# Graph attention on one core: row units put between masks and scores of a step

## The reference

```python
qkv = layer_norm(x, g1, be1) @ w_qkv
q, k, v = (qkv[:, 0], qkv[:, 1], qkv[:, 2])          # after reshape(n, 3, HEADS, HEAD_DIM)
scores = jnp.einsum('nhd,mhd->hnm', q, k) * SCALE
scores = jnp.where((adj != 0)[None, :, :], scores, -jnp.inf)
attn = jax.nn.softmax(scores, axis=-1)
out = jnp.einsum('hnm,mhd->nhd', attn, v).reshape(n, DIM)
x = x + out @ w_proj + b_proj
h2 = layer_norm(x, g2, be2)
return x + jax.nn.gelu(h2 @ w1 + b1) @ w2 + b2
```

## Time and profile before

| | |
|---|---|
| median of three runs | 1814.01 us (1806.6 to 1814.49) |
| profiled execution | 1812.5 us, its span 1810.7 us |
| granted TensorE clock over the span | 0.976 |
| TensorE matmuls | 1673.6 us, 92% |
| VectorE | 1421.2 us, 78% |
| ScalarE | 1300.8 us, 72% |
| GpSimd | 1179.4 us, 65% |
| chain that ended last | TensorE 71%, ScalarE 15%, issue 10%, VectorE 2% |

### The profile page before, as it was taken

How to read it: one execution, slowest core, us unless ns; L and a number is a source line. 1 busy time by engine, 2 the same in 40 slices (tenths; PEclk the granted TensorE clock), 3 DMA queues, 4 the chain that set the end, 5 groups by cost and what they waited for, 6 DMA issues and landing times.

```text
span 1810.7 us, 48122 instructions
## 1 busy us (share of the span) xinstructions
PE 1673.6 (92%) x17826; PEld 553.9 (31%) x17826; DVE 1421.2 (78%) x4495; ACT 1300.8 (72%) x1443; POOL 1179.4 (65%) x1113
## 2 busy tenths in 40 slices
PE   6989999999999999999999999999999999999985
PEld 3422222323223232323223232323223232233223
DVE  6888889877898779887888779887898778987601
ACT  4547777677776777777776877677776877777771
POOL 5944586568855787468855688458865688457441
PEclk9869999999999999999999999999999999999996
DMA  7710035202450035301360035300351024500000
GB/s 214 168 42 2 25 108 110 54 1 66 135 100 2 13 106 117 66 1 54 114 133 2 1 100 124 77 2 26 123 106 47 2 77 124 77 2 1 8 7 6
DMA packets 168846, 115.24 MB, mean 64 GB/s; under 512 B 139298, under 2 KB 149156, under 8 KB 168612
## 3 DMA queue, kind: packets, MB, share of 16 engines
q1 hardware_dynamic: 157860, 103.78, 23.7%
q10 hardware_dynamic: 10752, 8.39, 1.6%
HBM read 74.39 MB, written 4.19 MB: 43 GB/s over the span
## 4 chain that ended last, share of the span: by engine, by line
PE 71%; ACT 15%; issue 10%; DVE 2%; DMA 1%; POOL 0%; SPq 0%; ACTq 0%; DVEq 0%; POOLq 0%
PE pv_ps L1023 19%; PE ring_ps L960 14%; PE score_ps L1127 12%; PE score_ps L1112 12%; ACT probs L728 12%; PE score_ps L1046 2%; PE ring_ps L1080 2%; PE ring_ps L1071 2%; PE ring_ps L1056 2%; PE ring_ps L1062 2%; PE score_ps L1036 2%; PE score_ps L984 2%; ACT q_stack L612 1%; ACT hidden L689 1%; DMA adj_in<-adj 1%
## 5 line engine op out<-in xcount | busy, mean ns | idle before, releaser
L763 DVE CUSTOM_DVE_ANT_0 masked_out<-ring_ps,row_mask 128x512 bf16<-128x512 f32 x2048 | 1310.3, 687 | 163.2 <-PE ring_ps L960 129.4
L728 ACT ACTIVATE probs<-score_ps,score_scale 128x1024 f32<-128x1024 f32 x1024 | 1089.0, 1113 | 358.0 <-PE score_ps L1127 350.4
L517 POOL TENSOR_TENSOR probs<-probs,keep 128x1024 int32<-128x1024 int32 x256 | 604.4, 2362 | 324.3 <-ACT probs L728 313.3
L1023 PE MATMUL pv_ps<-probs,v_ones 128*17 128x512 f32 x4096 | 539.2, 599 | 0.5 <-POOL probs L517 0.4
L960 PE MATMUL ring_ps<-k_stack,q_stack 51*64 51x512 f16 x4096 | 493.3, 397 | 13.3 <-DVE row_max L763 12.8
L1127 PE MATMUL score_ps<-q_stack,k_stack 51*64 51x512 f16 x4096 | 373.5, 391 | 26.6 <-ACT probs L728 7.4
L1112 PE MATMUL score_ps<-mask_t,ident_bf 64*64 64x512 bf16 x3072 | 276.1, 387 | 60.9 <-ACT probs L728 14.6
L960 PEld LDWEIGHTS ring_ps<-k_stack,q_stack 51*64 51x64 f16 x4096 | 165.8, 104 | 454.7 <-DVE row_max L763 401.9
L1127 PEld LDWEIGHTS score_ps<-q_stack,k_stack 51*64 51x64 f16 x4096 | 116.9, 104 | 229.2 <-PE score_ps L1112 181.1
L763 DVE DVE_READ_ACCUMULATOR2_ANT row_max<- 128x1 f32 x2048 | 169.4, 83 | 0.0
L1112 PEld LDWEIGHTS score_ps<-mask_t,ident_bf 64*64 64x64 bf16 x3072 | 92.4, 105 | 211.3 <-ACT probs L728 114.1
(11 more groups left out here) (106 smaller groups left out, 969.6 us busy)
## 6 DMA issues: line engine op xcount, KB each, us to landing
adj_in<-adj SPq DMA_DIRECT2D x128, 512.0 KB, 4.1
xnT_dram<-attn ACTq DMA_DIRECT2D x8, 256.0 KB, 3.9
mask_t<-row_mask SPq DMA_TRANSPOSE x128, 3.4
xq<-xnT_dram ACTq DMA_DIRECT2D x8, 256.0 KB, 2.6
x_res<-x ACTq DMA_DIRECT2D x8, 256.0 KB, 4.4
out<-rows ACTq DMA_DIRECT2D x8, 256.0 KB, 2.6
w_sb<-L_gnn_w SPq DMA_DIRECT2D x2, 256.0 KB
probs<-x SPq DMA_DIRECT2D x1, 256.0 KB, 2.9
```

The source lines that it names most:

```text
L517: nc.gpsimd.tensor_tensor(view, view, keep[:, KEPT.index(m), :].unsqueeze(1).broadcast_to([128, 2, TILE]), ALU.mult).then_inc(probs_masked, 1)
L728: nc.scalar.activation(probs[:, (2 * g + n) % SLOTS, :], score_ps[:, half:half + 2, :].rearrange("p a n -> p (a n)"), ACT.Exp, scale=score ...
L763: nc.vector.tensor_tensor_reduce(out=masked_out[:, place % 3, :], in0=ring_ps[:, place % 3, :], in1=row_mask[:, j, ch * 512:(ch + 1) * 512 ...
L1023: last = nc.tensor.matmul(pv_ps[32 * k:32 * k + HD + 1, :], v_ones[:, block_of(g, b), 2 * p + a, :], probs[:, (2 * g + b) % SLOTS, a * TIL ...
```

## The change

Only the order of TensorE's instructions inside a step changes. Before, two row units stood first, then all masks and scores of both blocks, then two row units, then the values. Now the first masks stand first (masked step only), then two row units, first scores, second masks, two row units, second scores, values. Fills stay behind the values.

```diff
                 for g in range(STEPS):
+                    if c and not pool_step(g):
+                        masks(g, 0)
                     for x in range(UNITS // 2):
                         row(g, x)
-                    if c and pool_step(g):
+                    if c:
                         scores(g, 0)
                         masks(g, 1)
-                        scores(g, 1)
-                    elif c:
-                        masks(g, 0)
-                        masks(g, 1)
-                        scores(g, 0)
-                        scores(g, 1)
                     for x in range(UNITS // 2, UNITS):
                         row(g, x)
+                    if c:
+                        scores(g, 1)
                     if g < LAG and d:
                         weigh_values(i - 1, made_by(i - 1), STEPS - LAG + g)
```

## The result

The changed kernel takes 1893.29 us (median of 4 runs, 1891.82 to 1896.46) against 1814.25 us before; the ratio is 1.044, 95% interval 1.0421 to 1.046. Its profiled execution took 1896.46 us, with a span of 1894.7 us, 84.0 us more than the span of before. The forecast was 1897 us.

A forecast was written before the change was run, and what follows sets the result against it. Taken as bound by latency, with the row chain of 1.35 us a floor in each step. Plain-first steps +11, masked +63, fills -12, -9 and +31 sum to +84 us on 1814: 1898, told as 1897 us; range 1845 to 1932.

The forecast's parts named there:

- Bound: Each step: fourth row unit needs the first's bank, so it cannot start sooner than 1.35 us after the first.
- Part 1: Plain-first step: two row units between second masks and second scores save 0.24 us on paper, and ScalarE's wait there goes.
- Part 2: Before the fourth row unit: TensorE waits 0.65 us instead of 0.18 (masked step) or none; chain taken as 1.37 us.
- Part 3: Behind the fourth row unit: second scores now precede the values, 0.55 us to the values instead of 0.31 to 0.33.
- rival C: Second scores run beside the fourth row unit, 0.43 us to the values instead of 0.55: 1845 us; chance 0.13.
- Part 4: Masked step: first masks ahead of the first row units add 0.22 us no longer hidden under the row chain.
- The fills: 175 steps with other work between values: -12 us behind shift transpositions, -9 behind q or up projections, +31 in others.
- The ends: Stage without row units, paced by ScalarE, left at nothing (-3 to +3 us); start of the program unchanged.
- A sign that read wrong: Profile after, whole kernel: VectorE and ScalarE keep their busy time and lose share.
- A: Faster: fourth row unit isn't held, 0.24 us saved in about 240 plain-first steps, 58 us, 1756 us; chance 0.04.
- B: No change: the row chain takes what the masks gain, or VectorE's earlier start pays it back, 1814 us; chance 0.04.
- D: Clock: pauses of 0.65 us per step drop a tenth of the steps to 1.2 GHz, +115 us, 2010 us; chance 0.05.

The follow-up runs named there:

- Run 3: Changed kernel with VectorE's row maximum over 256 instead of 512 columns of each row unit: 1782.72 us, against the changed kernel's 1893 us.
- run 1: Kernel before with only the first masks of a masked step moved ahead of its first two row units: 1833.1 us, ratio 1.0106.
- run 5: Changed kernel with the second scores ahead of the fourth row unit instead of behind it: 1820.71 us, ratio 1.0042 to the kernel before.
- run 2: Kernel before with only the second scores of each step moved behind the last two row units: 1859.69 us, ratio 1.0257.
- run 9: Kernel before, changed order only behind q or up projections or shift transpositions without VectorE fill, and in the masked step ahead of such a transposition: 1798.99 us.
- run 6: Kernel before with the second scores between third and fourth row unit, first masks left behind the first two row units: 1805.5 us, ratio 0.9965.
- run 4: Kernel before with VectorE's row maximum over 256 instead of 512 columns of each row unit: 1770.95 us, ratio 0.976.

## Why the prediction was right, step by step

**Bound.** The row chain, 0.60 + 0.69 + 0.06 us from the first to the fourth row unit of a step, was named as a floor. It held: 425 of 480 steps after have the fourth unit between 1.32 and 1.38 us, none sooner. Run 3 shows that it is VectorE's duration that sets it: 0.27 us less of that, and the fourth unit comes 0.27 us sooner. The floor presumes that VectorE is free when the first row unit comes; runs 1, 3 and 5 show steps where it was not.

**Part 1, the masks' latency.** Right that it is gained (scores' waits for masks halved), right that it is worth nothing in a plain step, since the time is waited for the row chain instead. Wrong in a detail: waits of masks for ScalarE were said to shrink and stayed (94.7 against 94.4 us).

**Part 2, the cover.** 1.35 to 1.37 us measured, 1.37 taken.

**Part 3, what stands behind the late unit.** 0.55 us measured, 0.55 taken, and run 5 shows it alone: with the scores ahead of the fourth row unit it is 0.33 us again, and 73 us come back. The picture behind the number was not quite right. The four score matmuls don't all come 0.22 us behind the row unit: the group has a record of 0.61 us instead of 0.41. The two matmuls issued last, of which one carries the group's semaphore increment, start at 864.19 beside the row unit, and the two issued first 0.23 us later. So rival C's mechanism exists, but the values need the whole array and follow the later half; it saves nothing.

**Part 4, the first masks.** 0.24 to 0.25 us measured, 0.22 taken. Run 1 shows the part alone at +20 us, less than half of what run 2's part costs, because here the next step gets something back.

**The fills.** All three groups within 3 us of the forecast (-12 for -12, -8 for -9, +34 for +31). The reason given for the first was half of it; run 9 shows the rest.

**The ends.** Left at nothing, they gave -1 us behind the last row unit and some -3 us in the start. The start also differs between the other kernels with the whole row maximum: first values at 128.0 and 129.9 us in the two whose granted clock over the first 122 us was 0.89, at 130.4 to 134.3 us in the rest (0.84 to 0.87). This is why the profiled execution is 1896.5 us where steps alone say 1812.5 + 88 = 1900.5. The steps were 4 us above the forecast and the ends 4 us below it, so that both cancel is luck.

**A sign that read wrong.** VectorE and ScalarE were to keep their busy time. VectorE did within 11 us; ScalarE's rose by 45 us, by records that no longer overlap and not by more work.

**The rivals.** A is out, since no step has the fourth unit sooner than 1.32 us. B is out by the time and by the masked step's +0.42 us. C is out by the 0.55 us of part 3. D is out: granted clock 1.00 from 152 to 1780 us. The rule of the Trainium skill, "TensorE: Matmul & The Clock Gate", section "A second HAM failure mode: psum-queue depth-cycling", that short idle moments between groups of matmuls that cycle through PSUM banks can make the clock swing, is not borne out here: a pause of about 0.6 us in most steps left it at 1.00, the upper level.

## What to carry to other kernels

With a ring of n buffers between two engines, the use n places on can't start sooner than producer's latency + consumer's time + the way back, and later if the consumer has something else in hand. Measure this once (here 1.35 us for three banks) and put as much other work of the producer into that span as it holds; what stands behind the waiting instruction in the same queue is added in series. So the last unit of a burst belongs at the end, with everything that doesn't need it ahead of it. And an order need not be the same in every step: where another engine is late for its own reasons, the order that loses elsewhere can win.

## What was not expected of the hardware

Matmuls that use only half of the array's rows can start ahead of matmuls issued before them that wait for the other half. In the changed kernel two of the second scores do so by 0.23 us (part 3 above). In run 6 the queue is first scores x4, third row unit x2, second scores x4, fourth row unit x2:

```profile
886.34 0.62 PE L1127 MATMUL score_ps<-q_stack,k_stack 51*64 51x512 f16 x6
886.59 0.38 PE L960 MATMUL ring_ps<-k_stack,q_stack 51*64 51x512 f16 x2
886.80 0.38 PE L1127 MATMUL score_ps<-q_stack,k_stack 51*64 51x512 f16 x2
886.97 0.40 PE L960 MATMUL ring_ps<-k_stack,q_stack 51*64 51x512 f16 x2
```

Two of the second scores start together with the third row unit, 0.25 us behind the first scores, and the other two 0.21 us later. A row unit put alone between scores therefore costs its half 0.21 us and the other half nothing.

Runs 3 and 4 against the others also show that VectorE's custom reduction takes 422 ns for 256 columns and 687 ns for 512: about 1.04 ns a column and 0.16 us besides.
